# Experts 1 to 3 of a fused attention and expert FFN kernel: another order of the steps on ACT, DVE and POOL

## The reference

```
x = x + gat_2_layers(ctx, adj = layernorm(x), W0, a0, b0, W1, a1, b1)
x4 = layernorm(x).reshape(4, 128, 4, 512)            # b, g, e, h: row 4g+e goes to expert e
gate, up = split(x4[:, :, e] @ gate_up_proj[e])       # 512 -> 2 x 512, for e = 0..3
out[:, :, e] = (silu(gate) * up) @ down_proj[e]       # 512 -> 512
x = x + out
```

## Time and profile before

| | |
|---|---|
| median of 3 runs | 245.34 us (244.63 to 246.07) |
| the profiled execution's own time | 245.4 us |
| its span | 243.6 us |
| TensorE busy | 209.5 us (86%) |
| TensorE weight loads | 167.3 us (69%) |
| DVE busy | 150.0 us (62%) |
| POOL busy | 127.4 us (52%) |
| ACT busy | 101.1 us (42%) |

### The profile page before, as it was taken

One profiled execution on the slowest core, in us unless ns is written; L12 is line 12 of the kernel. 1 busy time (PEld: TensorE's weight loads), 2 busy tenths in 40 slices (PEclk: granted clock), 3 DMA queues, 4 the chain that ended last, 5 costly groups with the idle time before them and its releaser, 6 DMA issues.

```text
span 243.6 us, 2785 instructions
## 1 busy us (share of the span) xinstructions
PE 209.5 (86%) x927; PEld 167.3 (69%) x927; DVE 150.0 (62%) x275; ACT 101.1 (42%) x162; POOL 127.4 (52%) x105
## 2 busy tenths in 40 slices
PE   7450299889996989999999999999959999989990
PEld 3240278667785867888777888888748888868860
DVE  0203989999999945343769787568558657112360
ACT  2105778998893654111281520351343143212010
POOL 2000344996798568778255896505889410840100
PEclk9886569999999999999999999999999999999996
DMA  7999800644544397803526997933975002200014
GB/s 156 303 396 368 241 0 3 202 159 159 178 167 108 129 288 170 213 3 52 80 61 202 201 223 187 292 93 104 245 176 166 0 0 91 81 3 1 0 46 133
DMA packets 39906, 34.59 MB, mean 142 GB/s; under 512 B 13648, under 2 KB 30032, under 8 KB 39376
## 3 DMA queue, kind: packets, MB, share of 16 engines
q1 hardware_dynamic: 30976, 24.93, 32.4%
q0 software_dynamic: 2816, 4.20, 11.2%
q10 hardware_dynamic: 6096, 5.25, 7.3%
HBM read 25.97 MB, written 8.40 MB: 141 GB/s over the span
## 4 chain that ended last, share of the span: by engine, by line
PE 46%; DVE 21%; DMA 14%; issue 7%; POOL 7%; ACT 2%; ACTq 1%; POOLq 0%; DVEq 0%
PE bank L1598 27%; PE bank L1612 14%; DMA b_col<-in_L_xattn_b 7%; DMA x_sb<-y_table,ff_row 5%; POOL ff_row L775 4%; DVE top L1182 4%; DVE hexp L1163 4%; DVE found L1186 3%; DVE val L1176 2%; DVE hexp L1157 2%; DVE xstat L1194 2%; PE bank L1536 2%; DMA y_table<-val 2%; POOL x_sb L786 1%; PE bank L1581 1%
## 5 line engine op out<-in xcount | busy, mean ns | idle before, releaser
L1598 PE MATMUL bank<-acts,ring 128*128 128x512 f32 x288 | 66.8, 389 | 0.0
L1598 PEld LDWEIGHTS bank<-acts,ring 128*128 128x128 f32 x288 | 54.1, 188 | 11.2
L764 POOL TENSOR_TENSOR ring<-stage,ring 128x1024 fp32r<-128x1024 f32 x16 | 40.3, 2528 | 19.1 <-ACT ring L897 19.1
L1520 PE MATMUL bank<-wide,acts 128*128 128x512 f32 x192 | 45.4, 394 | 4.0 <-ACT bank L929 3.9
L1520 PEld LDWEIGHTS bank<-wide,acts 128*128 128x128 f32 x192 | 35.5, 188 | 13.1 <-ACT bank L929 5.9
L1612 PE MATMUL bank<-ring,wide 128*128 128x512 f32 x144 | 35.4, 395 | 3.5 <-issue 3.5
L770 POOL TENSOR_TENSOR acts<-hexp,acts 128x512 fp32r<-128x512 f32 x14 | 18.7, 1362 | 31.0 <-ACT acts L920 31.0
L1612 PEld LDWEIGHTS bank<-ring,wide 128*128 128x128 f32 x144 | 26.5, 188 | 9.6 <-issue 4.3
L786 POOL DMA_INDIRECT x_sb<-y_table,ff_row x16 | 26.4, 1651 | 8.9 <-DVE xstat L1194 4.9
L1506 PE MATMUL bank<-ctxT,W0p 128*128 128x512 f32 x48 | 16.0, 487 | 16.4 <-DVE ctxT L1146 13.1
L897 ACT CAST ring<-stage 128x1024 fp32r<-128x1024 f32 x24 | 24.5, 1056 | 7.7 <-DMA stage<-in_L_ffn_gate_up_proj 5.5
(11 more groups left out here) (85 smaller groups left out, 280.2 us busy)
## 6 DMA issues: line engine op xcount, KB each, us to landing
stage<-in_L_ffn_gate_up_proj SPq DMA_DIRECT2D x32, 256.0 KB, 3.8
x_sb<-in_x SPq DMA_DIRECT2D x4, 1024.0 KB, 10.3
stage<-in_L_ffn_down_proj SPq DMA_DIRECT2D x8, 512.0 KB, 4.1
y_table<-val SPq DMA_DIRECT2D x16, 256.0 KB, 3.3
out<-x_sb ACTq DMA_DIRECT2D x16, 256.0 KB, 3.6
ctx_xn<-in_ctx SPq DMA_DIRECT2D x4, 256.0 KB, 10.4
val<-in_ctx SPq DMA_DIRECT2D x1, 1024.0 KB
val<-in_L_xattn_W SPq DMA_DIRECT2D x4, 256.0 KB
```

Source lines behind the costliest of these rows:

```text
L764: nc.gpsimd.tensor_tensor(fills[f]["lo"], fills[f]["raw"], fills[f]["hi"].bitcast(F32), ALU.subtract).then_inc(w_lo, 1)
L1520: last = nc.tensor.matmul(bank[n % YB][:, :], hT[:, b % 2, c, w, t * P:(t + 1) * P], W1p[:, c, v, :], start=False, stop=(c == KC - 1 and j ...
L1598: last = nc.tensor.matmul(bank[4 + 2 * (c % 2) + half][:, :], ring[:, r % RING, w, col:col + P], xnT[:, e % 2, k, v, :], start=(k == 0 and ...
```

## The change

Nothing is added to or taken from the work; steps change their places in the streams of ACT, DVE and POOL. On ACT the weight pieces' high parts move in front of each silu, so that `inner_high(e, c)` follows `silu_of(e, c)` directly, and three of the four `turned_xn` move behind `inner_high(e, 3)`. On POOL the gathers go two by two between the low parts, and the inverse deviations for the next expert go behind `inner_low(e, 2)`. On DVE `x_stats` goes behind `outputs`, the statistics and `normalize` of the next expert go behind `inner(e, 2)`, `small_maxima` in front of it, `ctx_maximum` behind `w_low(14)`, the last `w_low` in front of `inner(e, 3)`, and the proof's `xmv` into expert 3. SyncE's and TensorE's streams are as they were.

```diff
@@ -864,28 +864,32 @@
             w_low(FIRST + 9)
             w_low(FIRST + 10)
             for e in range(1, E):
-                if e + 1 < E:
-                    for b in range(B):
-                        gather(b, e + 1)
-                inner_low(e, 0)
                 for r in (6 * e + 6, 6 * e + 7):
                     if r < PER_E * E:
                         w_low(FIRST + r)
+                inner_low(e, 0)
+                if e + 1 < E:
+                    gather(0, e + 1)
+                    gather(1, e + 1)
+                else:
+                    pool.wait_ge(xmv_made, B * E)
+                    inverse_std(xmv, slice(0, B * E), xrstd, rstd_no(E, 0))
                 inner_low(e, 1)
+                if e + 1 < E:
+                    gather(2, e + 1)
+                    gather(3, e + 1)
+                if 6 * e + 9 < PER_E * E:
+                    w_low(FIRST + 6 * e + 9)
+                inner_low(e, 2)
                 if e + 1 < E:
                     x2_inverse_std(e + 1, 0)
                     x2_inverse_std(e + 1, 1)
-                if 6 * e + 9 < PER_E * E:
-                    w_low(FIRST + 6 * e + 9)
-                inner_low(e, 2)
+                if 6 * e + 10 < PER_E * E:
+                    w_low(FIRST + 6 * e + 10)
                 if e == E - 2:
                     pool.wait_ge(small_made, 5)
                     nc.gpsimd.partition_all_reduce(allmax[:, :], rowmax[:, :], P, RMAX).then_inc(all_made, 1)
                     nc.gpsimd.partition_all_reduce(allsum[:, :], rowsum[:, :], P, RSUM).then_inc(all_made, 1)
-                    pool.wait_ge(xmv_made, B * E)
-                    inverse_std(xmv, slice(0, B * E), xrstd, rstd_no(E, 0))
-                if 6 * e + 10 < PER_E * E:
-                    w_low(FIRST + 6 * e + 10)
             unless_sure(pool, general.gpsimd)
 
         @block.scalar
@@ -1109,31 +1113,31 @@
             turned_xn(1, 2)
             turned_xn(1, 3)
             for e in range(1, E):
-                store(e - 1)
-                silu_of(e, 0)
                 for r in (6 * e + 6, 6 * e + 7):
                     if r < PER_E * E:
                         w_high(FIRST + r)
+                store(e - 1)
+                silu_of(e, 0)
                 inner_high(e, 0)
-                silu_of(e, 1)
                 if 6 * e + 8 < PER_E * E:
                     w_high(FIRST + 6 * e + 8)
+                silu_of(e, 1)
                 inner_high(e, 1)
-                silu_of(e, 2)
                 if 6 * e + 9 < PER_E * E:
                     w_high(FIRST + 6 * e + 9)
+                silu_of(e, 2)
                 inner_high(e, 2)
+                for r in (6 * e + 10, 6 * e + 11):
+                    if r < PER_E * E:
+                        w_high(FIRST + r)
                 silu_of(e, 3)
                 if e + 1 < E:
                     turned_xn(e + 1, 0)
-                    turned_xn(e + 1, 1)
                 inner_high(e, 3)
                 if e + 1 < E:
+                    turned_xn(e + 1, 1)
                     turned_xn(e + 1, 2)
                     turned_xn(e + 1, 3)
-                for r in (6 * e + 10, 6 * e + 11):
-                    if r < PER_E * E:
-                        w_high(FIRST + r)
             store(E - 1)
             unless_sure(act, general.scalar)
 
@@ -1448,37 +1452,40 @@
             turned_low(1, 3)
             w_low(FIRST + 11)
             for e in range(1, E):
+                outputs(e - 1)
                 if e + 1 < E:
                     for b in range(B):
                         x_stats(e + 1, b)
-                outputs(e - 1)
                 inner(e, 0)
+                if 6 * e + 8 < PER_E * E:
+                    w_low(FIRST + 6 * e + 8)
                 if e == 1:
                     ctx_maximum()
-                if 6 * e + 8 < PER_E * E:
-                    w_low(FIRST + 6 * e + 8)
+                if e == E - 1:
+                    for t in range(B * E):
+                        nc.vector.bn_aggr(xmv[:, t, :], xstat[:, t // E, t % E, :]).then_inc(xmv_made, 1)
                 inner(e, 1)
+                if e == 1:
+                    small_maxima()
+                inner(e, 2)
                 if e + 1 < E:
                     for b in range(B):
                         x2_stats(e + 1, b)
                         x2_moments(e + 1, b)
                     for b in range(B):
                         normalize(e + 1, b)
-                inner(e, 2)
-                if e == 1:
-                    small_maxima()
-                if e == E - 2:
-                    for t in range(B * E):
-                        nc.vector.bn_aggr(xmv[:, t, :], xstat[:, t // E, t % E, :]).then_inc(xmv_made, 1)
-                if e == E - 1:
+                else:
                     check_rows()
+                if 6 * e + 11 < PER_E * E:
+                    w_low(FIRST + 6 * e + 11)
                 inner(e, 3)
+                if e + 1 < E:
+                    turned_low(e + 1, 0)
                 inner_low(e, 3)
                 if e + 1 < E:
-                    for b in range(B):
-                        turned_low(e + 1, b)
-                if 6 * e + 11 < PER_E * E:
-                    w_low(FIRST + 6 * e + 11)
+                    turned_low(e + 1, 1)
+                    turned_low(e + 1, 2)
+                    turned_low(e + 1, 3)
             outputs(E - 1)
             dve.wait_ge(sure_counted, 1)
             nc.vector.tensor_copy(flag[:, :], bank[4][0:1, 0:1]).then_inc(flag_made, 1)
```

## The result

| | before | after |
|---|---|---|
| median | 245.7 us (4 runs, 244.63 to 246.98) | 249.26 us (4 runs, 248.15 to 250.45) |
| ratio of after to before, 95% interval | | 1.0143 (1.0074 to 1.0213) |
| the profiled execution's own time, its span | 245.4, 243.6 us | 249.5, 247.7 us |
| first gate matmul of expert 1 | 131.10 | 130.30 |
| from there to `project_down(1, 3)` | 31.64 us | 40.25 us |

The lower part of the table is the whole difference of the two spans: -0.8 + 8.6 - 4.0 + 0.3 = +4.1 us. The change loses 8.6 us in expert 1 and wins 4.0 in experts 2 and 3. The -0.8 is chance: nothing ahead of expert 1 was changed, and over all the traces of this case its first gate matmul starts between 130.06 and 131.35.

A forecast was written before the change was run, and what follows sets the result against it. TensorE, busy 86% of the span, was taken as the bound, with 3.8 us of holes to win. Expert 1 +6.65, experts 2 and 3 -2.7 and -1.1: +2.85 on 245.4, so 248.2 us, range 244.7 to 251.0.

The forecast's parts named there:

- The hole at `turn_xn(2, 0)`: Expert 1: TensorE waits 4.1 us there because `inner(1, 2)` comes later, with statistics and `normalize` now behind it.
- the start of the chain: Expert 1: `ctx_maximum`, which releases the reloads and fill 15, ends 2.3 us later, at 142.6 instead of 140.29.
- its length: Expert 1, from `ctx_maximum` through the reloads to `small_maxima`: unchanged, since the DMA work in the stretch is the same.
- The stall: SyncE's queue, expert 1: the 4.43 us at the third W1 piece comes back; sign: one piece over 4 us to issue.
- Rival (a): Expert 1: fewer gathers ahead shorten the reload chain by 3.3 us, 244.9; chance alone 0.12. Against it: two gathers fall into the chain.
- two waits on one chain: Expert 1: `small_maxima` and `w_high(15)`, ahead of `silu(1, 2)`, both wait for DMA after `ctx_maximum`; `inner(1, 2)` ends at 158.5.
- The port: End of expert 1: POOL's `w_low(16)` slows the last two `normalize` to 3.06 us, as in the old trace.
- Rival (b): End of expert 1: `normalize(2, 2)` gets in ahead of `w_low(16)`, `project_down(1, 3)` starts at 167.4, total 246.2; chance alone 0.09.
- The clock: Behind the 4.1 us hole the clock falls, costing at most 0.9 us; lasting over `project_down(1, 3)`: 251, chance 0.08.
- The hole of about 2 us: Sign in expert 1: TensorE idle 1.9 us ahead of `turn_xn(2, 2)`, waiting for `inner(1, 3)`.
- -3.8 us in experts 2 and 3: The holes ahead of `project_down(2, 0)` and `(3, 0)` go, winning 2.7 and 1.1 us.
- So it is ACT's order: Expert 2: the 2.53 us hole comes from `inner_high(2, 0)` standing behind two `w_high`, not from the four gathers.

The follow-up runs named there:

- new1_old23: The kernel before with the new order in expert 1 only, the old one in experts 2 and 3: 249.67 us against 244.45, ratio 1.022.
- port_free: The changed kernel, but in expert 1 POOL's `w_low(16)` waits until all four `normalize` are done: 248.85 us in one execution, 244.45 before.
- ctx_first: The changed kernel with `ctx_maximum` ahead of `w_low(14)` again: 244.22 us in one execution (244.45 before); repeated with ten executions (suffix _r) 245.4 us, ratio 1.006.
- small_late: The changed kernel with `small_maxima` behind the last `turned_low` of expert 1: 248.68 us in one execution, 244.45 before.
- w15_late: The changed kernel with piece 15's high part behind `inner_high(1, 2)` and its low part behind the deviations: 250.9 us in one execution, 244.45 before.
- both_late: The changed kernel with `small_maxima` at the end of expert 1 and piece 15 behind `inner_high(1, 2)`: 246.92 us against 244.45 before, ratio 1.015.
- act_only2: The kernel before with `w_high(18)` and `(19)` ahead of the stores in expert 2: 246.59 us in one execution, 244.09 before.
- tail_only: The kernel before with `w_high(16)`, `w_high(17)` and DVE's `w_low(17)` earlier in expert 1: 241.49 us against 244.45, ratio 0.990.
- old1_new23: The kernel before with the old order in expert 1, the new one in experts 2 and 3: 241.34 us against 244.45, ratio 0.987.

## Why the prediction was right, and where it wasn't

- **The sum.** Forecast +2.85 us (248.2), measured +3.6 in the medians and +4.1 in the profiles. Expert 1 cost 8.6 us where 6.65 were forecast, and 0.8 us of that miss is hidden in the profiles' total by expert 1 starting earlier, which is luck.
- **The hole at `turn_xn(2, 0)`: mechanism right, size short.** Forecast 4.1, measured 5.6; as a delay of `turn_xn(2, 0)` against the first gate matmul it is 5.7, so 1.6 of the 1.95 us missed in expert 1 lie here. Of its terms the start of the chain was right (2.3 forecast, 2.5 us measured). The term that was mis-sized is its length: I took it as unchanged, "since the DMA work in the stretch is the same", and it grew by 1.7 us (from the end of `ctx_maximum` to `small_maxima` 11.9 us before, 13.6 after; 13.0 and 13.4 in new1_old23 and port_free). The stall on which I let it hang did not come back: the longest of the four W1 pieces took 2.23 us to issue, not over 4, and the four together 1.15 us less than before. What grew lies behind them: 1.75 us in the issues of W0 and the vectors (one of them 2.26 us, 0.69 before), 1.1 us in the landing of the last.
- **Why the chain grew.** The gathers are the likely reason, though no run moves them alone. Before, all four were issued between 132.4 and 139.6, ahead of the chain, and the engines were busy with them (share 1.11 and 0.93 in the two stretches from 136 to 140); now they are issued from 138.9 to 148.2, the engines are nearly idle from 136 to 142 (0.13, 0.02, 0.00), and all of the gathers' data falls into the chain. Rival (a), a shorter chain, was wrong for the changed kernel, and its own counter-argument (the two other gathers fall into the chain) was the better one; with the W1 pieces issued ahead of most of the gathers the chain is 10.7 and 10.5 us (ctx_first, ctx_first_r).
- **That two waits on one chain hold `inner(1, 2)`**: shown by small_late, w15_late and both_late together.
- **The port: right.** 3.04 against 3.06 forecast. Rival (b) didn't come by itself; port_free, which forces that order, shows that it would have been worth 0.6 us and not 2, since the half clock takes its place.
- **The clock: right that it would fall, and that `project_down(1, 2)` hides it**: 0.28 us are left between the end of `inner(1, 3)` at 169.03 and `turn_xn(2, 2)` at 169.31. The hole of about 2 us that I had named there as a sign did not appear, because the slower `project_down(1, 2)` filled it.
- **-3.8 us in experts 2 and 3: the amount was right (4.0), the account of the holes was not.** The step that failed is "So it is ACT's order". The 2.53 us hole ended at ACT's two `w_high`, but act_only2 shows that their place was worth 1.0 us, and tail_only shows that with the old order inside both experts the holes are gone once the tail of expert 1 is cleared. The whole expert began late on DVE, behind `w_low(17)`; I had followed the wait back by two steps, and the row that decides, DVE's `w_low` at 165.59, is several steps further back. That the amount came out all the same is partly luck: the changed kernel has two remedies, and each alone is enough (old1_new23 has only the new order in experts 2 and 3, new1_old23 only that in expert 1, and tail_only nothing of it but the tail). The hole of expert 3 goes with the first one in tail_only, with the all-reduces in their old place in the stream: POOL's next step behind them comes 3.2 us into expert 3 instead of 4.9, some 1 us of that by the earlier start and 0.8 by a shorter idle behind them (6.79 us, 7.57 before).
- **What the change would have been worth.** Its good part is worth 3 us (old1_new23, tail_only); the bad part is the order inside expert 1 only, where two of the moved steps wait for DMA and a third, `ctx_maximum` behind `w_low(14)`, starts that DMA later.

## What to carry to other kernels

A step that waits for a DMA has a price in every place where it has something behind it: before moving it ahead of work on the critical chain, look not at how long it takes but at when its data lands, and at what starts that transfer. Where a hole's releaser is itself late, follow it back until an engine is found that was busy and not waiting; here it stood at the end of the expert before, and three moved instructions were enough. And an order that is right in the loop's later rounds may be wrong in the first one, where one-off work shares the queues.

## What the runs showed of the hardware that I had not expected

- **The same hole can cost the clock or not.** Holes of 2.53 us (before) and 2.62 us (ctx_first_r) left the granted clock at 1.00; one of 2.47 us in act_only2 was followed by 0.50 over more than 2 us (twelve matmuls 4.45 us instead of 3.0). First a stretch behind the hole of ctx_first_r, then two of act_only2, columns as above:

```profile
161.00:162.00 1.00, 1.00 (x8) 0.89 (x7) 1.00 (x1) 0.59 (x1) 1.00 (x1) 1.00 0.00 0
...
214.00:215.00 1.00, 0.12 (x1) 0.15 (x1) 0.00 (x0) 0.00 (x0) 1.00 (x2) 0.79 0.00 0
215.00:216.00 1.00, 1.00 (x3) 0.81 (x4) 0.00 (x0) 0.00 (x0) 1.00 (x1) 0.50 0.06 16
```

  The Trainium skill (TensorE: Matmul & The Clock Gate, Part 1) says that the monitor behind the clock runs free of the kernel's start, so that the point at which the clock changes varies. These rows fit that; no run here shows that it is the reason.
- **DVE can stand behind two instructions of POOL.** `w_low(20)` took 6.19 us in act_only2 and ended 1.1 us behind the second of POOL's two `w_low`. In the kernel before, the same `w_low(20)` took 3.32 us beside the same two, so that it got in between them, and it began 0.15 us behind the first of them in both; what decides is open.
- **The all-reduces cost far more than their rows.** They show 0.39 and 0.53 us in the kernel before, but POOL idles 5.5 to 6.1 us ahead of the first in all twelve traces and 6.8 to 7.6 us behind the second in the four with work ready there. The Trainium skill (GPSIMD Engine Reference, section 2.1) names about 6 us for loading the code of a newly loaded kernel of that engine at its first call, with no instruction of its own in the profile. The idle time ahead of the first agrees with it in size; that it is this load no run shows, and what the time behind the second is stays open.
